# Expert weights of tiles 1 to 7 by eight row transfers, routing seven units sooner, the next rows' norm and high part on ScalarE

## The reference, cut to what matters

```python
x = x + _L1_ffn_ref(_layernorm(x), centroids, expert_biases, Ws_up, Ws_down, W_up, W_down)

def _L1_ffn_ref(x, ...):                      # E = 64 experts of width 64, TOP_K = 8
    shared = silu(xf @ Ws_up) @ Ws_down
    aff = xf @ centroids.T
    _, idx = top_k(aff + expert_biases, 8)
    w = sigmoid(aff[idx]);  w = w / (sum(w) + 1e-08)
    cw = zeros(T, E).at[tokens, idx].add(w)
    h = silu(einsum('td,edf->etf', xf, W_up))
    y = einsum('etf,efd->etd', h, W_down)
    return shared + einsum('etd,te->td', y, cw)
```

## Time and profile before

| what | value |
|---|---|
| median of 3 runs | 1028.47 us (1028.38 to 1029.89) |
| the profiled execution, its own time | 1029.46 us |
| its span, first to last instruction | 1027.6 us |
| TensorE clock granted, mean over the span | 0.955 |
| PE / DVE / ACT / POOL busy | 92% / 80% / 68% / 47% |
| last stage | from 608 us to the end |

### The profile page before, as it was taken

How to read it: one execution, slowest core, us unless ns; L and a number is a source line. 1 busy time by engine, 2 the same in 40 slices (tenths; PEclk the granted TensorE clock), 3 DMA queues, 4 the chain that set the end, 5 groups by cost and what they waited for, 6 DMA issues and landing times.

```text
span 1027.6 us, 20126 instructions
## 1 busy us (share of the span) xinstructions
PE 948.5 (92%) x6082; PEld 755.7 (74%) x6115; DVE 821.2 (80%) x1938; ACT 701.5 (68%) x1394; POOL 478.4 (47%) x550
## 2 busy tenths in 40 slices
PE   3676998999789999999999989999999999999997
PEld 2555998999667777677767657777777777777786
DVE  6888776777778888888887668888887888797865
ACT  4663554555468777877777667777777777687875
POOL 3278781007456565655644304444444444443443
PEclk8665999999789999999999999999999999999999
DMA  8994332222211100110010019292919292939392
GB/s 257 404 386 161 109 91 63 66 69 68 60 24 32 32 22 22 32 32 22 27 27 12 1 32 218 65 230 62 232 50 228 56 226 60 211 73 210 79 211 57
DMA packets 69156, 110.99 MB, mean 108 GB/s; under 512 B 16784, under 2 KB 54707, under 8 KB 64963
## 3 DMA queue, kind: packets, MB, share of 16 engines
q1 hardware_dynamic: 64080, 100.72, 37.5%
q0 software_dynamic: 4384, 8.99, 2.9%
q10 hardware_dynamic: 594, 0.09, 0.0%
HBM read 70.90 MB, written 38.86 MB: 107 GB/s over the span
## 4 chain that ended last, share of the span: by engine, by line
PE 62%; DVE 16%; DMA 7%; issue 5%; ACT 5%; SPq 2%; POOL 1%; DVEq 0%; POOLq 0%; ACTq 0%
DMA cwB<-cwd 5%; PE ps L2496 4%; PE ps L2478 3%; PE ps L2480 3%; PE ps L2479 3%; PE ps L2498 3%; PE ps L2497 3%; PE ps L2199 3%; PE ps L2309 3%; PE ps L2331 3%; PE ps L2303 3%; PE ps L2348 3%; DVE nm L1919 2%; PE ps L2177 2%; PE ps L2179 2%
## 5 line engine op out<-in xcount | busy, mean ns | idle before, releaser
L927 POOL TENSOR_TENSOR hl<-h,hh 128x512 fp32r<-128x512 f32 x128 | 167.4, 1308 | 257.0 <-ACT hh L1238 257.0
L1238 ACT ACTIVATE hh<-h 128x512 fp32r<-128x512 f32 (+1 forms) x264 | 165.3, 626 | 36.1 <-DVE h L2004 33.1
L2004 DVE TENSOR_TENSOR h<-ps,cwB 128x512 f32<-128x512 f32 x192 | 130.0, 682 | 45.7 <-ACT ps L1227 33.2
L1919 DVE TENSOR_REDUCE nm<-ps 128x4 f32<-128x512 f32 (+1 forms) x128 | 116.4, 952 | 38.1 <-PE ps L2331 35.9
L1227 ACT ACTIVATE ps<-ps 128x512 f32<-128x512 f32 x192 | 111.6, 581 | 35.7 <-PE ps L2480 34.4
L2478 PE MATMUL ps<-xh,wh 128*128 128x512 f32 x256 | 103.8, 405 | 0.0
L2496 PE MATMUL ps<-hh,wh 128*128 128x512 f32 x256 | 102.9, 402 | 0.6 <-POOL hl L927 0.6
L2011 DVE TENSOR_TENSOR hl<-h,hh 128x512 fp32r<-128x512 f32 (+1 forms) x136 | 96.0, 706 | 8.7 <-ACT hh L1238 7.6
L2479 PE MATMUL ps<-xl,wh 128*128 128x512 f32 x256 | 100.3, 392 | 0.0
L2480 PE MATMUL ps<-xh,wl 128*128 128x512 f32 x256 | 100.2, 391 | 0.0
L2498 PE MATMUL ps<-hh,wl 128*128 128x512 f32 x256 | 100.1, 391 | 0.0
(11 more groups left out here) (367 smaller groups left out, 2679.3 us busy)
## 6 DMA issues: line engine op xcount, KB each, us to landing
cwB<-cwd SPq DMA_DIRECT2D x32, 1536.0 KB, 14.7
ys<-zfill SPq DMA_DIRECT2D x13, 1536.0 KB, 22.6
cwd<-cwS SPq DMA_DIRECT2D x64, 96.0 KB
xb<-xs SPq DMA_DIRECT2D x72, 64.0 KB
ys<-yb SPq DMA_DIRECT2D x72, 64.0 KB
x_res<-in_L_attn_x_dram SPq DMA_DIRECT2D x4, 512.0 KB, 6.5
wst<-in_L_ffn_W_up_dram SPq DMA_DIRECT2D x32, 64.0 KB, 2.1
wst<-in_L_ffn_W_down_dram SPq DMA_DIRECT2D x32, 64.0 KB, 1.9
```

The lines of the kernel that those rows point to most:

```text
L927: pool.tensor_tensor(hl4[:, slot(u), :], h4[:, slot(u), :], hh4[:, slot(u), :].bitcast(F32), op=ALU.subtract).then_inc(u_hlp, 1)
L1238: act.activation(hh4[r, slot(u), :], h4[r, slot(u), :], ACT.Copy).then_inc(u_hh, 1)
L1919: ins = dve.tensor_reduce(nm[:, u, 4 * g:4 * g + 4], o, axis=AX.X, op=ALU.max, negate=True)
L2004: dve.tensor_tensor(h4[:, slot(u), :], first, second, op=ALU.mult).then_inc(u_h, 1)
```

## The change

**Weights.** In tiles 1 to 7 no unit uses the spreading matmul: all 32 units read `cwB`. The load is cut into eight pieces of 4 units (1024 KB each) in four buffers. Tile 0 keeps the spreading matmuls for units 1 to 8 and loads pieces 2 to 7. Storing takes four transfers a tile, each of 16 partitions written eight times, in place of eight of 48 partitions. SP's order becomes: piece 4, the finished tile, pieces 5 to 7, the stores of the next tile, its pieces 0 to 3. The low-part columns of the weights and their three DVE operations, and the ACT copy to `cwT`, stay only for tile 0.

**Routing sooner.** The turn goes from unit 11 to 6, the copy to unit 7, the logits from 14 to 11, the SiLU of the logits from 17 to 13, the turn and copy of the weights from 30 to 23. DVE's steps go from units 12 to 27 to units 9 to 20. The statistics go from unit 3 to unit 24 and POOL's rstd to unit 25. The finished tile is transposed into its own bank, so that the turn no longer waits for u_y; PE no longer waits for d_cw at a tile's first unit, but at the turn.

**Norm and high part.** From the rows of tile 2 on, ACT makes the norm in four operations at its units 1 to 4 (scale and bias per partition; POOL makes the bias nb4 with two more small operations), and for tiles 1 to 7 ACT makes the high part at unit 8.

```diff
-        NPC, NBUF = 4, 3
-        G = NB // NPC
+        NPC, NBUF = 8, 4
+        G = NP2 // NPC
+        P0 = NS // G
...
+        def spread_unit(t, u):
+            return isinstance(t, int) and t == 0 and 0 < u <= NS
+        def buffer_of(piece):
+            return (piece + P0) % NBUF
...
+        def up_bank(t, u):
+            if isinstance(t, int) and t == 0:
+                return u % 3 if u <= NS else (u - NS - 1) % 5
+            return u % 5
...
-        X4_TURN, X4_LOGITS, X4_SILU, X4_SPREAD = 11, 14, 17, 30
+        X4_TURN, X4_COPY, X4_LOGITS, X4_SILU, X4_SPREAD = 6, 7, 11, 13, 23
+        X4_NORM = 1
+        STATS_AT = 24
...
+            def store_weights(t):
                 sp_.wait_ge(d_cw, t + 1)
-                for r in range(CWR):
-                    sp_.dma_start(cwd[t % 2, :, :, r, :].rearrange("k h x -> (k h) x"), cwS[0:EB, :]).then_inc(rows_out, 16)
-                sp_.wait_ge(rows_out, 16 * CWR * (t + 1))
+                for j in range(G):
+                    sp_.dma_start(cwd[t % 2, :, :, :, j * TT:(j + 1) * TT].rearrange("k h r t -> (k h) r t"),
+                                  cwS[j:HB:G, :].unsqueeze(1).broadcast_to([HB // G, CWR, TT])).then_inc(rows_out, 16)
+                sp_.wait_ge(rows_out, 16 * G * (t + 1))
...
+            def early_pieces(t):
+                store_weights(t)
                 for piece in range(NBUF):
-                    if t > 0:
-                        last = max(k for k in range(NPC) if k % NBUF == piece)
-                        sp_.wait_ge(u_h, (t - 1) * NP2 + NS + (last + 1) * G)
+                    sp_.wait_ge(u_h, (t - 1) * NP2 + (piece + NBUF + 1) * G)
                     load_rows(t, piece)
+            def late_piece(t, piece):
+                sp_.wait_ge(u_h, t * NP2 + (piece - NBUF + 1) * G)
+                load_rows(t, piece)
...
             for t in range(T // TT):
                 if t > 0:
+                    late_piece(t, NBUF)
                     sp_.wait_ge(u_y, t)
                     sp_.dma_start(out_tok[...], y4[...]).then_inc(o_out[(t - 1) % 2], 16)
-                rows_again(t)
+                for piece in range(NBUF + (1 if t > 0 else P0), NPC):
+                    late_piece(t, piece)
                 if t + 1 < T // TT:
-                    spread_rows(t + 1)
+                    early_pieces(t + 1)
...
 (POOL, x4_rstd)
+                pool.tensor_scalar(nb4[:, p, :], mv[:, p, :, 0], -1.0, None, ALU.mult).then_inc(act_d, 1)
+                pool.tensor_tensor(nb4[:, p, :], nb4[:, p, :], rstd[:, p, :], op=ALU.mult).then_inc(d_rs, 1)
...
 (ACT)
+            def x4_norm(n, p, k):
+                if k == 0:
+                    act.wait_ge(d_rs, 2 * n)
+                ins = act.activation(xm4[:, k:k + 1, :], x_res[:, ds(n * SUB + k, 1), :], ACT.Identity,
+                                     scale=rstd[:, p, k:k + 1], bias=nb4[:, p, k:k + 1])
+            def x4_high(n, p):
+                act.activation(xh4[:, p, :], x4_bank(n)[:, :], ACT.Copy).then_inc(d_Tc, 1)
...
+                    if X4_NORM <= u < X4_NORM + SUB and N and before is not None:
+                        x4_norm(t + 1, 1 - p, u - X4_NORM)
...
 (DVE)
-            STEP_AT = (6, 12, 13, 15, 15, 16, 17, 18, 19, 20, 21, 22, 23, 24, 24, 25, 26, 27)
+            STEP_AT = (1, 8, 9, 12, 12, 13, 14, 15, 16, 16, 17, 18, 18, 19, 19, 20)
-                    own.done(dve.tensor_tensor(g4[:, 5, :, 0:EP], g4[:, 4, :, 0:EP], inverse...))
-            def low_weights(): ...
...
 (PE)
-                    pe.wait_ge(d_cw, t + 1)
+                    if isinstance(t, int) and t == 0:
+                        pe.wait_ge(d_cw, 1)
-                if u > 0 and not broadcast_unit(u):
+                if spread_unit(t, u):
...
-            def out_T(t):
+            def out_T(t, p):
-                    ins = pe.transpose(bank[6][...], oT4[...], ident[:, :])
+                    ins = pe.transpose(bank[5 + 2 * p][...], oT4[...], ident[:, :])
```

More of the change, by code:

```diff
@@ L297, in bass_two_layers @@
         xl4 = sb("xl4", [P, 2, TT], F32R)
-        cwT = sb("cwT", [P, 2, TT], F32R)
+        cwT = sb("cwT", [P, TT], F32R)
         selr = sb("selr", [P, EP, F2], F32R)
@@ L459, in wait_bank @@
                     return
-                earlier = [(a, v, t - 1) for a, v, k in BANKS_USED if k == BANKS_USED[n][2]]
+                earlier = [(a, v, t - 1) for a, v, k in banks_used(t - 1) if k == here[n][2]]
             a, v, t_of = earlier[-1]
@@ L639, in rows_again @@
-            def rows_again(t):
-                for piece in range(NBUF, NPC):
-                    sp_.wait_ge(u_h, t * NP2 + NS + (piece - NBUF + 1) * G)
-                    load_rows(t, piece)
-            spread_rows(0)
+                for j in range(G):
+                    sp_.dma_start(cwd[t % 2, :, :, :, j * TT:(j + 1) * TT].rearrange("k h r t -> (k h) r t"),
+                                  cwS[j:HB:G, :].unsqueeze(1).broadcast_to([HB // G, CWR, TT])).then_inc(rows_out, 16)
+                sp_.wait_ge(rows_out, 16 * G * (t + 1))
@@ L1108, in x4_weights @@
                 if not (isinstance(n, int) and n == 0):
-                    act.wait_ge(rows_out, 16 * CWR * n)
-                act.activation(cwT[:, p, :], x4_bank(n)[:, :], ACT.Copy)
+                    act.wait_ge(rows_out, 16 * G * n)
+                else:
+                    act.activation(cwT[:, :], x4_bank(n)[:, :], ACT.Copy)
                 act.activation(cwS[:, :], x4_bank(n)[0:HB, :], ACT.Copy).then_inc(d_cw, 1)
@@ L1766, in norm @@
                 def norm():
+                    if not (isinstance(n, int) and n <= 1):
+                        return
                     dve.wait_ge(d_rs, n + 1)
@@ L1773, in high @@
                 def high():
-                    dve.wait_ge(d_Tc, n + 1)
+                    if not first:
+                        return
+                    dve.wait_ge(d_Tc, 1)
                     apart(dve, dve_passed)
@@ L1778, in low @@
                 def low():
-                    own.need(1)
+                    if first:
+                        own.need(1)
+                    else:
+                        dve.wait_ge(d_Tc, 2 * n + 1)
                     dve.tensor_tensor(xl4[:, p, :], flat(xnT4[:, :, :]) if first else x4_bank(n)[:, :], xh4[:, p, :].bitcast(F32),
@@ L2043, in dve_tile @@
                         last_attended(u)
-                    if u == 3 and S:
+                    if u == STATS_AT and S:
                         x4_stats(t + 2, p)
@@ L2252, in _, with x4_turned @@
             pe.wait_ge(c_const, 1)
-            def x4_turned(n, free):
+            def x4_turned(n):
                 pe.wait_ge(d_xn, n + 1)
-                if free is not None:
-                    pe.wait_ge(u_y, free)
+                if not (isinstance(n, int) and n == 0):
+                    pe.wait_ge(d_cw, n)
                 for k in range(SUB):
@@ L2262, in x4_logits @@
             def x4_logits(n):
-                pe.wait_ge(d_Tc, n + 1)
+                pe.wait_ge(d_Tc, 1 if isinstance(n, int) and n == 0 else 2 * n)
                 if not (isinstance(n, int) and n == 0):
@@ L2520, in pe_tile @@
                     if u == 7 and before is not None:
-                        out_T(before[0])
+                        out_T(before[0], 1 - p)
                     if u == X4_TURN and N:
-                        x4_turned(t + 1, t if before is not None else None)
+                        x4_turned(t + 1)
                     if u == X4_LOGITS and N:
```

134 lines of the change are left out of this document (65 added, 69 removed).

## The result

| | before | after |
|---|---|---|
| median, us | 1029.67 (1028.38 to 1031.75, 5 runs) | **1037.50** (1036.82 to 1040.41, 5 runs) |
| ratio to before | | 1.0081, 95% interval 1.0068 to 1.0094 |
| profiled execution, us | 1029.46, span 1027.6 | 1038.08, span 1036.3 |

The forecast was 1013.3 us with a range of 1007 to 1023. It was wrong in size and in sign, 24 us off; a slower kernel had a chance of 0.08 in it.

A forecast was written before the change was run, and what follows sets the result against it. TensorE was taken as the bound (304.3 of 311.3 us busy in tiles 1 to 6). Terms -12.7 - 5.1 - 3.0 + 4.9 + 0.7 = -15.2 us took 1028.47 to a median of 1013.3 us, range 1007 to 1023.

The forecast's parts named there:

- TensorE is the bound ... matmuls taken away there should come back in full, unless something else becomes late: Tiles 1 to 7: TensorE limits, so leaving out 56 spreading matmuls of 0.227 us each gives -12.7 us.
- Logits, -5.1: Logits two units after the low part instead of one: TensorE's 6.5 us wait there shrinks, 0.2 a tile left, -5.1 us.
- The loop through unit 9: Tiles 2 to 5: late transfer at unit 9 delays result, turn, logits, routing and next loads; of 4.1 us excess, -3.0.
- VectorE's squeeze, +4.9: Units 12 to 20: routing in nine units puts VectorE 3.3 us behind; 0.7 us charged to each of seven tiles, +4.9.
- ScalarE at the first units, +0.7: Units 1 to 8: with norms and high part ScalarE needs 11.8 us against TensorE's 11.6, +0.7 us in all.
- Cover gone, a fraction of a us a tile; priced 0: Statistics at unit 24, GpSimd's rstd and two small operations delay one low part of unit 27; priced 0.
- Weights through DRAM, 0: Tile start: first load lands 3.0 us after it, h of unit 1 needs it at 3.3; fits, priced 0.
- The rival, which begins at 5.4 us a load: SP's load queue becomes the bound and slower than before, from 5.4 us a load; 1050 us, chance 0.08.
- Tile 0 changes little: Tile 0 keeps its spreading matmuls, so its time was expected to change little.
- tile starts 49 to 50 us apart: Sign that the forecast is right: successive tiles of the last stage start 49 to 50 us apart.
- the + 5 beside the + 7: Slow end of the added bounds, -12.7 - 2.3 - 1.0 + 7 + 5 = -4.0 us; +7 is VectorE's squeeze at its upper end.
- ScalarE's own upper end of 1.3 us a tile: Units 1 to 8: upper end of ScalarE's delay, 1.3 us a tile, from VectorE's norm showing 2.01 us for four.

The follow-up runs named there:

- b_nospread: The kernel before with only the 56 spreading matmuls of tiles 1 to 7 left out, units 1 to 8 missing from its result; ratio to before 0.9983.
- a_best: The changed kernel with tiles 2 to 5 written out, nb4 declared last, statistics at unit 4 and tile 1's norm at unit 3; ratio to before 0.9881.
- b_unrolled: The kernel before with tiles 2 to 5 written out instead of the hardware loop; ratio to before 0.9948.
- the pair of tile 0 fences: Two changed-kernel traces, unchanged (1.0105) and with pieces 1 to 3 of tile 4 held (1.0025): tile 0's norm took 2.08 us beside GpSimd, 1.11 alone.
- a_stats4: The changed kernel with the statistics back at unit 4 and GpSimd's rstd at unit 5; ratio to before 1.0047.
- a_best24: a_best with the routing steps spread over one unit more and the weights' turn at unit 24 instead of 23; ratio to before 0.9949.
- the pair on one chip: The changed kernel unchanged (1.0105, tile 0 55.8 us) and with tile 1's norm at unit 3 instead of 1 (1.0056, tile 0 52.9 us).
- a_unrolled: The changed kernel with tiles 2 to 5 written out, so that no engine jumps back; ratio to before 0.9967.
- a_hold4: The changed kernel with SP issuing pieces 1 to 3 of tile 4 only after that tile's first h; ratio to before 1.0025.

## Why the prediction was wrong, step by step

**"TensorE is the bound ... matmuls taken away there should come back in full, unless something else becomes late": it held for the changed kernel, but not for the reason given.** A busy share of 98% of the tile says that an engine has little idle time, not that the others have more. In the kernel before, the matmuls alone gave 1.9 us of 12.7 (b_nospread), because the chain of load, h, y and turn met TensorE at unit 11. The sign was in the rows quoted: VectorE waited for loaded weights 6.3 us in four tiles and the turn for y 1.0. In the changed kernel that chain is gone, and the term is there: units 1 to 11 take 15.28 us where they took 16.35, although each unit is 0.035 longer by its distances and the turn lies inside them now; in a_best, 15.00.

**Logits, -5.1: the wait went as said** (6.5 to 0.8 us), and it counts. Units 11 to 15, which held the turn and the logits, take 6.80 us where they took 8.58 (7.85 unrolled). Up to unit 15 the change is 2.85 us a tile faster than before, 2.1 faster than b_unrolled.

**"The loop through unit 9", -3.0: half of the cause.** Tiles 2 to 5 took 208.9 us, unrolled 204.7, and that difference of 4.2 is all of the excess that the step shared out. In tiles 3 and 5 two thirds of it do sit where the step says: from unit 11 to 12 they take 2.40 and 2.46 us, tiles 2 and 6 take 1.72. In tile 4 it is the jump's delay (see there), and in all four some 0.3 us at the end of routing. But without the hardware loop all three go, so all hang on it, and the change kept the loop. Why the loop lengthens tiles 2, 3 and 5 as well, where nothing jumps back, stays open.

**VectorE's squeeze, +4.9: right, if a little small.** In the changed kernel TensorE's units 20 to 23 take 1.2 us a tile more than they need, where units 24 to 30 before took 0.5: 0.7 a tile. In a_best, with the shorter distance, units 15 to 31 take 23.97 us against 22.84 in b_unrolled: 1.1 a tile.

**ScalarE at the first units, +0.7: no wait of TensorE for it is in the trace.** The norm costs ScalarE 0.48 us apiece, 24 of them:

```profile
L1120 ACT ACTIVATE xm<-x_res,nb,rstd 128x128 f32 (+1 forms) x24 | 11.6, 482 | 0.0
```

The step weighed the Trainium skill, SBUF — State Buffer, "Who interferes with whom", by which VectorE's two-port operations and GpSimd exclude each other for a whole instruction. The pair of tile 0 fences agrees with it: 2.08 against 1.11 us. The step also said that no row shows the norm beside GpSimd. The trace had it: VectorE's norm of 2.01 us started at 878.92, a low part of GpSimd of 1.29 us at 878.79, so about one of the 2.01 can be put down to GpSimd.

**"Cover gone, a fraction of a us a tile; priced 0": mis-sized.** The four operations were counted as one rstd and two small ones. They take 2.6 us, and TensorE pays for them between units 31 and 32: 2.45 us where a_stats4 takes 1.40, 1.0 in each of tiles 2 to 5 and 0.8 in tile 1, 5 us in the traces and 3.5 by the ratios. GpSimd's mean load of 132 in 311 us was read where the place counts: it has a low part of 1.3 us to make every two units, 2.8 us, and four operations of 2.6 us do not fit in between.

**Weights through DRAM, 0: right for what it asked, with little to spare.** From the first store to the first load it was 6.5 us, not 5.0 (753.2 to 759.7, tile 3 starting at 764.8). Three loads issued from 759.7 on took 7.1, 11.3 and 15.4 us, 4.7 to 4.8 apart with the 0.6 between issues, as forecast 4.7. The rival, which begins at 5.4 us a load, is out. The Trainium skill, DMA: Bandwidth & Descriptors, "Bandwidth", has 6.15 us for 1 MB, in a table of transfers issued by GpSimd; the trace does not agree for loads queued by SP, and the measurement decides. The first lands 2.0 us after the tile starts (3.0 forecast), and VectorE's wait for it is 0.4 us once. The DMA share of 0.84 in tile 3 and a_best24 say how near the limit is.

**Two terms were missing, and the first is the step that failed most.** "Are the first loaded rows there at unit 1?" was all that the step on the loads asked before it priced them 0. It did not ask what else is held up by transfers that start 5 us before a tile does: 10.4 us at tile 4 (61.8 against 51.4), with the clock's lower level in it. And no step asked what a new buffer does to the addresses of the others: 0.4 us a tile, 2 to 3 in all.

**"Tile 0 changes little": failed**, 5.0 us by the two traces, 2.9 of it by the pair on one chip. Its norm was moved from unit 6 to unit 1 by the same table that serves the other tiles, but there it is still on VectorE. With that, the placement and the statistics mended (a_best), tile 0 takes 50.9.

The sum can be set beside the spans of the two profiled executions, 1027.6 and 1036.3: +8.7 us where -15.2 was forecast, 23.9 missed. The jump has 10.4 of it, tile 0 5.0, the operations behind the statistics 5.0 in tiles 1 to 5, and the placement 2.4 as an estimate (0.4 in six tiles). The stage start and the tail came out 2.2 better, by nothing that was forecast. That leaves 3.3 us for the loop that was kept and the larger squeeze. The parts come from single traces and overlap, as a wait of one engine covers what another loses.

Taken out together they leave 0.9881, about 12 us below before, where 15 was forecast: the six tiles 1 to 6 of a_best take 299.2 us, a mean of 49.9, and "tile starts 49 to 50 us apart" was the forecast's own sign. So the mechanism for a plain tile was right in the main, and what failed is what the change set off around it. Part of the 12 us is the unrolling, which the kernel before can have as well; against it unrolled (0.9948, in another group) the change's own idea is worth 0.7%, or 7 us.

One number of the prediction's upper bound has no working: the + 5 beside the + 7. ScalarE's own upper end of 1.3 us a tile would be 9.1.

## What to carry to other kernels

A busy share of 98% doesn't promise that work taken off that engine comes back: count the other chains to the same point before giving the term in full, and compare kernels from one unit's start to the next, as a gain and the wait that eats it can lie ten units apart. A run that leaves the work out by itself tests the kernel it is made from; where the change also clears the chain that would eat the gain, it says too little. Moving a transfer earlier moves it beside something else; at a hardware loop's jump that is most likely the fetch of code, so look at what is in flight where the loop turns. Put small new buffers behind the old ones, and small operations of GpSimd where its results have slack, not where it is idle on average.

## What the runs showed of the hardware

- 32 bytes more or less ahead of the operands change the distance of 512-column matmuls from 0.227 to 0.233 us, with everything else equal; 64 bytes gave 0.229 to 0.231.
- At a hardware loop's jump an engine's next instruction can come late, and later the more transfers are in flight: ScalarE's 7 us late (7.8 to 8.5 after the tile's start against 1.0) with several weight loads, 2.7 with one, not at all unrolled; VectorE's 1.6 us late with none (5.5 against 3.9), 6.0 with four DRAM copies. That it is the fetch of code is the likely reading, not shown by itself.
- The profile's releaser can be the wrong one: at the jump a delay of VectorE was put down to ScalarE, and the landing of a weight load was called "issue".
- Four 128x128 norms of VectorE take 1.11 us alone and 2.08 when a low part of GpSimd starts among them.
- After a stop of 4.8 us TensorE's matmuls came 0.43 us apart for some 8 us, after one of 1.8 or 2.0 for seven matmuls; in a_unrolled, a_hold4 and a_best tile 4 has none of that (granted clock 1.00).
